# Two attentions' TensorE order written out over eight steps: score pairs in runs of three, three and two, with one projection piece beside a value product

## The reference

```python
# L0 (a bias on q, k, v; the scale is 1/16)
q = (xm @ Wq + bq).reshape(B, S, NH, DH)
k = (xm @ Wk + bk).reshape(B, S, NH, DH)
v = (xm @ Wv + bv).reshape(B, S, NH, DH)
q = q / DH
w = jax.nn.softmax(jnp.einsum('bqhc,bkhc->bhqk', q, k), axis=-1)
y = jnp.einsum('bhqk,bkhc->bqhc', w, v).reshape(B, S, H)
x = x + g_msa[:, None, :] * (y @ Wo + bo)
# L2 (no bias, rotary embedding, the scale is 1/4)
q = q * cos + rotate_half(q) * sin
k = k * cos + rotate_half(k) * sin
attn = jax.nn.softmax(jnp.einsum('bhnd,bhmd->bhnm', q, k) * scale, axis=-1)
out = jnp.einsum('bhnm,bhmd->bhnd', attn, v)
```

## Time and profile before

| | us |
|---|---|
| median of 3 runs | 930.33 |
| lowest, highest | 926.66, 932.41 |
| the profiled execution, its own time | 927.77 |
| its span on the core | 925.6 |
| mean granted TensorE clock, share of full | 0.989 |

### The profile page before, as it was taken

How to read it: one execution, slowest core, us unless ns; L and a number is a source line. 1 busy time by engine, 2 the same in 40 slices (tenths; PEclk the granted TensorE clock), 3 DMA queues, 4 the chain that set the end, 5 groups by cost and what they waited for, 6 DMA issues and landing times.

```text
span 925.6 us, 14715 instructions
## 1 busy us (share of the span) xinstructions
PE 878.1 (95%) x5294; PEld 539.3 (58%) x5294; DVE 587.9 (64%) x916; ACT 518.9 (56%) x955; POOL 468.7 (51%) x614
## 2 busy tenths in 40 slices
PE   5999999999989999998999999999999999999997
PEld 3453444444347779776878775444444433687874
DVE  4687887788895366554533277878777886234323
ACT  2226878776784444444364441677866778744331
POOL 4393565564748645447544424748255016665330
PEclk9979999999999999999999999999999999999999
DMA  7565584666212030123214136546636531100001
GB/s 231 153 160 163 155 248 121 183 173 186 85 57 91 1 134 1 36 72 139 79 48 180 12 95 173 154 127 184 177 112 200 138 108 58 38 14 1 23 24 45
DMA packets 67087, 101.30 MB, mean 109 GB/s; under 512 B 19644, under 2 KB 30984, under 8 KB 66632
## 3 DMA queue, kind: packets, MB, share of 16 engines
q1 hardware_dynamic: 58584, 86.90, 31.6%
q0 software_dynamic: 5920, 10.90, 4.6%
q10 hardware_dynamic: 2512, 2.58, 1.1%
HBM read 64.65 MB, written 35.02 MB: 108 GB/s over the span
## 4 chain that ended last, share of the span: by engine, by line
PE 78%; DVE 10%; ACT 4%; issue 4%; POOL 3%; DMA 0%; SPq 0%; DVEq 0%; POOLq 0%; ACTq 0%
PE PS L1151 13%; PE PS L715 12%; PE PS L689 12%; PE PS L1133 12%; PE PS L644 5%; PE PS L700 4%; PE PS L625 3%; PE PS L620 3%; DVE U L877 3%; ACT PH L779 2%; PE PS L456 2%; PE PS L657 2%; PE PS L633 1%; PE PS L474 1%; PE PS L1269 1%
## 5 line engine op out<-in xcount | busy, mean ns | idle before, releaser
L877 DVE TENSOR_REDUCE U<-PS 128x2 f32<-128x1024 f32 x256 | 307.8, 1220 | 55.3 <-PE PS L700 53.7
L779 ACT ACTIVATE PH<-PS 128x512 f32<-128x512 f32 x512 | 275.4, 605 | 87.8 <-PE PS L689 84.8
L689 PE MATMUL PS<-UR 50*128 50x512 f32 x512 | 187.4, 456 | 9.3 <-ACT PH L779 4.6
L700 PE MATMUL PS<-UR 48*128 48x512 f32 x512 | 190.9, 469 | 5.4 <-DVE U L877 4.7
L1199 POOL TENSOR_TENSOR PHR<-PH,PHR 128x512 fp32r<-128x512 f32 x96 | 124.1, 1296 | 118.6 <-ACT PHR L1189 118.6
L689 PEld LDWEIGHTS PS<-UR 50*128 50x128 f32 x512 | 79.2, 186 | 147.2 <-ACT PH L779 84.6
L1151 PE MATMUL PS<-UR,PHR 128*128 128x256 f32 x768 | 158.6, 290 | 4.1 <-POOL PHR L1199 4.0
L715 PE MATMUL PS<-PH,U 128*32 128x512 f32 x1024 | 137.2, 608 | 0.3 <-ACT PH L779 0.3
L1151 PEld LDWEIGHTS PS<-UR,PHR 128*128 128x128 f32 x768 | 124.6, 189 | 21.5 <-issue 18.5
L1151 PE MATMUL PS<-W2R,PHR 128*128 128x256 f32 x384 | 108.1, 282 | 0.0
L1188 ACT ACTIVATE PH<-PS,col 128x512 f32<-128x512 f32 x64 | 43.9, 687 | 93.5 <-PE PS L1133 93.5
(11 more groups left out here) (254 smaller groups left out, 1351.2 us busy)
## 6 DMA issues: line engine op xcount, KB each, us to landing
UR<-d_parts SPq DMA_DIRECT2D x112, 192.0 KB, 4.2
d_parts<-UR SPq DMA_DIRECT2D x42, 256.0 KB
d_parts<-UR POOLq DMA_DIRECT2D x40, 256.0 KB, 5.4
d_o<-U SPq DMA_DIRECT2D x32, 256.0 KB, 2.9
U<-in_L_cond_W_dram SPq DMA_DIRECT2D x8, 1024.0 KB, 7.6
W<-in_L_cond_W_dram SPq DMA_DIRECT2D x24, 256.0 KB, 3.3
U<-d_o SPq DMA_DIRECT2D x32, 128.0 KB
U<-d_rec SPq DMA_DIRECT2D x16, 256.0 KB
```

What stands on the lines that cost most here:

```text
L689: self.close(pe.matmul(dst, KP[g // 2][r:r + SROWS + 2, j, kt * P:(kt + 1) * P], QP[g // 2][r:r + SROWS + 2, j, :], start=True, stop=True) ...
L700: ins = pe.matmul(bank(2 + (w + 2) % 4), QP[g // 2][r:r + SROWS, j, qt * P:(qt + 1) * P], KP[g // 2][r:r + SROWS, j, :], start=True, stop= ...
L779: nc.scalar.activation(PH[:, m % 2, j, :], self.where("ST", n), ACT.Exp).then_inc(self.a_free, 1)
L877: v.tensor_reduce(mx[:, G % 2, :].rearrange("p (r c) -> p r c", r=2)[:, :, c // 2], PS[:, 2 + (w + 1) % 4:4 + (w + 1) % 4, :], AX.X, ALU.m ...
```

## The change

Three things are edited; no instruction is added or taken away.

1. Value products. They move from behind step 4m+7 to a pattern of eight steps: product 2k-2 is issued at step 8k ahead of its score pair, and product 2k-1 at step 8k+2 behind its pair. From step 226 on (`LONE`) the places are as before. So between value products lie pairs 8k, 8k+1, 8k+2 and then pairs 8k+3 to 8k+7.
2. Pieces. `Q`, `K` and `V` at steps with n mod 8 = 2 move two steps earlier (`piece`), onto 8k, where they stand ahead of product 2k-2. Those with n mod 8 = 6 stay, and so do `PJ`, `M`, `RQ` and `RK`. The second `T` of a batch, and its `XL`, move four steps earlier to the place of the first.
3. `M` and `MROW` of group 0 move two steps later, to -13 and -12.

```diff
+LONE = NSTEP - LOOK + 2
...
+    def piece(n):
+        return n - 2 if 0 <= n < LONE and n % 8 == 2 else n
...
-            put((-90, -36)[b] + i if b < 2 else o - 40 + 4 * i, "T", b, i)
+            put((-90, -36)[b] + i if b < 2 else o - 40, "T", b, i)
             if b >= 2:
-                put(o - 39 + 4 * i, "XL", b, i)
+                put(o - 39, "XL", b, i)
...
-                    put(at, c, b, 2 * half + part)
+                    put(piece(at), c, b, 2 * half + part)
...
-            put(-18 + 4 * t if first else o + (18 if b == 3 else 10) + 4 * t, "V", b, t)
+            put(piece(-18 + 4 * t if first else o + (18 if b == 3 else 10) + 4 * t), "V", b, t)
...
-        put(16 * G - (13 if G else 15), "M", G, 0)
-        put(16 * G - (12 if G else 14), "MROW", G, 0)
+        put(16 * G - 13, "M", G, 0)
+        put(16 * G - 12, "MROW", G, 0)
...
+            def values(self, pe, m):
+                if 0 <= m < NG * 4:
+                    b, g, kt = m // 16, m // 4 % 4, m % 4
+                    pe.wait_ge(self.a_free, self.scored(4 * m + 3))
...
+                    if n % 8 == 0 and n < LONE:
+                        self.values(pe, (n - 8) // 4)
                     if 0 <= n < NSTEP:
...
-                    if n % 4 == 3 and 0 <= (n - 7) // 4 < NG * 4:
-                        m = (n - 7) // 4
...
+                    if n % 8 == 2 and n < LONE or n % 4 == 3 and n >= LONE:
+                        self.values(pe, (n - 6) // 4)
```

More of the change, by code:

```diff
@@ L670, in spin @@
                               start=True, stop=True)
+            def values(self, pe, m):
+                if 0 <= m < NG * 4:
+                    b, g, kt = m // 16, m // 4 % 4, m % 4
+                    pe.wait_ge(self.a_free, self.scored(4 * m + 3))
+                    if m == 0 and self.a == 0:
+                        pe.wait_ge(mod_ready, 2)
+                    if kt == 0:
+                        self.wait_read(pe, "V", b, TT - 1)
+                        if m:
+                            pe.wait_ge(self.o_free, NG * self.a + m // 4)
+                    for j in range(4):
+                        ins = pe.matmul(PS[32 * j:32 * j + 32, 6, :], Vt[b % 2][:, kt, 4 * g + j, :], PH[:, m % 2, j, :],
+                                        start=(kt == 0), stop=(kt == 3))
+                    ins.then_inc(self.pv_done, 1)
             def pe(self, pe):
```

## The result

| | before | after |
|---|---|---|
| median, us | 929.35 (4 runs) | 941.09 (4 runs) |
| lowest, highest | 926.66, 932.41 | 940.46, 946.69 |
| the profiled execution | 927.77 | 940.46 |
| its span | 925.6 | 938.3 |
| mean granted TensorE clock in it | 0.989 | 0.979 |

The ratio is 1.0132, with 1.0100 to 1.0164 as its interval: slower by 1.3%. The kernel before has one more run here than in the table ahead of the prediction.

What follows compares the result with a forecast made beforehand. Bound: TensorE's order (78% of the chain), then three banks, then VectorE's reductions. The profiled 927.77 plus 3.8 (middle), 0.3 (early T, XL) and 2.3 (lead-in) gave 934.2, or 936.7 against the median; forecast 935.5, range 927 to 942.

Steps and rivals of the forecast that it cites:

- The middle, +3.8: Steps 4 to 220 of both attentions: bank and reduction waits outweigh saved runs, +2.0 in a=0 and +1.8 in a=1.
- the steps walked: Steps 4 to 220 of both attentions, each instruction started at the latest of spacing, bank reader and semaphores; sum +3.8.
- the split pair's reduction: Periods without a piece: the reduction of pairs 8k+2 and 8k+3, parted by a value product, delays TensorE; 5.54 for 5.23.
- ScalarE's bank for the piece at 8k+6: The piece, fourth taker behind a value product, waits for the exponential until 1.18 behind pair 8k+3: +0.27 per such period.
- One sign to look for: Q and K periods without M: piece at 8k+6 starts 1.18 behind pair 8k+3, period 6.6 or so; 6.3 without waits.
- The lead-in of a=1, +2.3: Before a=1's first pair: three saves issued ahead of MROW cost +3.0, less 0.7 for VectorE working off its backlog.
- XL and T early, +0.3: Where T and XL move earlier, XL's halves end 6.4 behind T and Q comes 6.3 behind; +0.3 for four cases.
- The direct step from piece to value product: A piece directly ahead of a value product costs what it costs ahead of a pair; the step takes 0.91.
- The lead-in of a=0, said 0: Before a=0's first pair: it starts near 63.51 as before; 0, bounds -0.3 and +0.5.
- Rival (c): Lead-in of a=1: saves ahead of MROW cost over 5.2, making the kernel slower by more than 1%; 940.3 against the median; 20%.
- The two rules of the Trainium skill: Tiling-mode changes drain TensorE (alone: all 12.2 gained); emptying PSUM may become the bottleneck (nothing gained).

Runs made afterwards that it cites:

- e3_save_behind: Kernel after with the first save of batch 1 one step later, behind MROW in SyncE's queue: median 941.09 against 930.44 for the kernel before, ratio 1.0102.
- e1_lead_only: Kernel before with only M and MROW of group 0 moved to -13 and -12: median 937.26 against 930.44, ratio 1.0073.
- e2: Kernel after with M and MROW of group 0 back at -15 and -14: median 938.97 against 930.44 for the kernel before, ratio 1.0082.
- e6: Kernel before with value products behind 8k+7 and 8k+2, pieces at 8k and 8k+5, only in periods with two pieces: median 933.26 against 928.29, ratio 1.0068.
- e7: Kernel before with M of groups 1 to 15 one step later, behind the value product: median 932.71 against 930.44, ratio 1.0006.
- e8: Kernel before with the statistics of step 212 spread over steps 184, 192, 200 and 208: median 929.55 against 928.29, ratio 1.0023.
- e9: Kernel before with M of groups 1 to 15 and batch 3's statistics one step later, step 212's statistics spread: median 923.86 against 928.41, ratio 0.9952.

## Why the prediction was right or wrong

**The middle, +3.8: near in size, and right in both causes.** Over the steps walked (4 to 220) the traces show +1.33 and +2.02, 3.35 together. Part of that agreement is luck: steps 4 to 12 of a=0 took 0.86 less, with a shorter stretch at 1.2 GHz in the kernel after. From step 12 to 220 it is +2.19 and +2.11, 4.3 together. By the groups of steps that the prediction names:

| steps | walked, a=0 | measured | walked, a=1 | measured |
|---|---|---|---|---|
| 4 to 36 | 0.0 | -0.75 | -0.7 | -0.65 |
| Q and K (36 to 60, 100 to 124) | +1.3 | +1.29 | +1.2 | +1.24 |
| 60 to 68, 124 to 132 | -0.9 | -0.96 | +0.5 | +0.52 |
| 68 to 100 | +0.7 | +0.78 | +0.2 | +0.14 |
| 132 to 164 | +0.3 | +0.06 | 0.0 | -0.14 |
| five periods without pieces | +1.3 | +1.60 | +1.3 | +1.60 |
| 180 to 196 | -0.7 | -0.68 | -0.7 | -0.70 |

Sixteen steps of Q and K were said to take 13.67 and took 13.63. Of the two causes, the split pair's reduction (where there is no piece) is shown by the halved reductions; ScalarE's bank for the piece at 8k+6 is read from the timeline, and the halved reductions only rule out VectorE there. One sign to look for was named wrongly: the periods of Q and K without M take 6.87 and not 6.6, for the finished group's copy falls in them too; the sum had its 0.30, the sentence on what would show it had not.

**The middle, what the walk left out.** Four of the five periods without pieces took +0.57 together; the fifth, steps 212 to 220, took +1.03, with the statistics of step 212 on VectorE. Steps 220 to 228 were not walked: +0.55 in a=0 and as much in a=1. So it is 4.45 over steps 4 to 252 of both, and 5.41 over steps 12 to 252. The statistics cost about 1 us before (their spreading gave 0.97 back in the old order). In the new order they cost at most an estimated 2.5, the 0.97 and the 1.57 added; part of the 1.57 is the order's own, for with halved reductions these steps still took 0.74 more (12.49 against 11.75), and no run spread the statistics in the new order.

**The lead-in of a=1, +2.3: the term that was mis-sized.** The place, the three saves and their cause were right; e3_save_behind shows it. The size was 4.68. MROW's last issue came 2.7 later (24.59 instead of 21.89), near the 3.0 taken; but the DMAs also took longer to land: the first pair starts 6.56 behind the last issue, where it was 4.57. The prediction put all the delay on the issues and took none for the landing; and it then took off 0.7 for VectorE's catching up, which no section shows. Across kernels the sum of both parts varies: +2.25 in e1_lead_only, which shares the order of the queue.

**Behind that wait.** Steps 0 to 12 of a=1 took 1.16 longer; the first 5.4 of their 11.2 us were at 1.2 GHz. No term of the sum stood for it.

**The other small terms.** XL and T early, +0.3: the steps where Q of batches 2 and 3 begins (28 to 36, 92 to 100) changed by 0.03 at most, so nothing. The direct step from piece to value product took what was said, 0.90 to 0.91 (107.12 to 108.02 in the trace of after). The lead-in of a=0, said 0: +0.89 in this pair of traces, but over the kernels with the old lead-in it lies between 22.8 and 27.0, and over the three with the new one between 25.6 and 28.6, so one pair of traces can't tell it.

**Rival (c), and why the loss passed 1%.** Rival (c) needed over 5.2 in the lead-in of a=1, after VectorE's catching up. 4.68 came there, and 5.84 with steps 0 to 12 behind it; but the last 1.16 were partly the clock's, and MROW's issues did not slow down as that rival had it (2.76 for the four, and not 1.34 each). The rest of the way past 1% stands beside a lower clock. A straight line with one slope and one height for each kernel, laid by least squares through 132 executions of nine kernels here (all but the two with halved reductions), gives 5.5 us for each 0.01 of the mean granted clock, and at equal clock, in us against the kernel before (a standard error of 0.6 to 1.0 each):

| e1 lead-in | e2 middle | after | e3 | e6 | e7 | e8 | e9 |
|---|---|---|---|---|---|---|---|
| +3.4 | +6.0 | +8.0 | +4.2 | +3.1 | +0.1 | -0.7 | -5.6 |

The kernel after has 8.0 at equal clock, by this estimate probably within 1% (9.3), though its error doesn't exclude more. The measured 11.7 has some 3.7 more, and the mean clock of the kernel after was 0.978, where the 63 executions of the kernel before had 0.986. At equal clock e3_save_behind is 3.8 below the kernel after, as its shorter lead-in (by 4.48) has it.

That the waits themselves bring the falls is not shown. They stand in or behind waits in the traces (the 6.40 before step 0 of a=1, the two at step 216), but not at each such wait: of the stretches behind step 216, three of six have 1.2 GHz in the new order (after, e2, e3), two of eight in the old one with the statistics whole (before, e1, e6, e7), none of four with them spread (e8, e9). And e8_stats_spread had no better clock over its executions. So it is partly luck that the time fell inside the range: neither the clock, nor steps 220 to 228, nor the landing stood in the sum, and together they brought it within 0.9 of the high end.

**The two rules of the Trainium skill** ("TensorEngine Tiling (Array Packing)", Key Properties and PSUM Bottleneck) both agree with the traces: something is there to be saved, 0.19 for a run, and the emptying of PSUM took more than was saved (1.18 to the fourth taker, 0.27 more than three pairs take). By the first alone 12.2 would have come.

## What to carry to other kernels

When an order is changed to save changes of mode on an engine, count the takers of each bank, and look for pairs that a longer instruction now splits: with three banks and the first free again after 1.18 us, a fourth taker gave back 0.27, more than the saved 0.19. A small DMA for which a stage's first instruction waits is issued ahead of bulk saves in the same queue, and priced with its landing. A walk of the order has to take in every task of the other engines up to the last period: the largest loss of the middle lay in the two periods where this one left out a task and then stopped.

## What the runs showed of the hardware

The same kernel's time spreads with the granted clock, and the falls move about: the kernel before ran from 924.3 to 939.4 us at mean clocks of 0.994 and 0.973. A wait of 0.86 and one of 0.38 or 0.39 close behind it, in a stream that was otherwise full, at step 216 of a=0, were followed by a stretch at 1.2 GHz in the profiled executions of e2_middle_only and e3_save_behind (steps 220 to 228 +4.39 and +4.28 against the kernel before), and by none in that of the kernel after. Waits of 0.47 and 0.40 in a=1 of e1_lead_only, in the old order, were followed by one too. So a change that shortens fixed stretches by 2 us can leave the median where it was (e8_stats_spread), and one that adds a wait can cost more than it lasts (e1_lead_only: 2.25 in the lead-in, 6.8 in the median, 3.4 at equal clock).

Four small DMAs behind three saves took 2.76 to issue, with the first pair 6.6 behind them, in one kernel, and 4.55 and 3.1 in another with the same order of the queue; what decides between the two was not tried.
